# Top-2 experts: up weights copied four tiles ahead, rows transposed six and gathered nine tiles ahead

## What is computed

```python
gate_logits = xf @ gate_w.T
weights, indices = jax.lax.top_k(gate_logits, TOP_K)
weights = jax.nn.softmax(weights, axis=-1)
combine = jnp.zeros((N, E)).at[jnp.arange(N)[:, None], indices].add(weights)
out = jnp.zeros_like(xf)
for e in range(E):
    h = jax.nn.silu(xf @ w1[e].T) * (xf @ w3[e].T)
    y = h @ w2[e].T
    out = out + combine[:, e:e + 1] * y
```

## Time and profile before

| what | value |
|---|---|
| median of 3 runs | 778.28 us (776.01 to 778.66) |
| profiled execution, its own time | 781.1 us |
| its span, first to last instruction | 779.3 us |
| mean granted TensorE clock | 0.787 of full |
| busy, PE / PEld / DVE / ACT / POOL | 68% / 54% / 50% / 45% / 45% |
| the top-2 loop, first gather to last scatter issued | 527.4 to 753.6 us |
| read-back, weighing and store behind it | to 779.3 us |

### The profile page before, as it was taken

One profiled execution on the slowest core, in us unless ns is written; L12 is line 12 of the kernel. 1 busy time (PEld: TensorE's weight loads), 2 busy tenths in 40 slices (PEclk: granted clock), 3 DMA queues, 4 the chain that ended last, 5 costly groups with the idle time before them and its releaser, 6 DMA issues.

```text
span 779.3 us, 12795 instructions
## 1 busy us (share of the span) xinstructions
PE 526.4 (68%) x4449; PEld 419.5 (54%) x4449; DVE 389.9 (50%) x1030; ACT 346.9 (45%) x731; POOL 350.3 (45%) x343
## 2 busy tenths in 40 slices
PE   4999732215394755059999989756787878878750
PEld 2445531211153634037777768745787877867750
DVE  5365657788520112398999998582111111111117
ACT  1112135534331121037777773305665756666645
POOL 2000000000268887347888873005666666667630
PEclk9999855556787687558999995556998989999985
DMA  9701146000045463720000002343111111111129
GB/s 302 317 27 28 40 86 162 0 0 0 17 125 116 95 143 35 177 49 2 3 3 3 3 2 69 82 101 106 45 45 41 42 42 45 41 42 48 39 70 284
DMA packets 65245, 56.05 MB, mean 72 GB/s; under 512 B 10176, under 2 KB 59200, under 8 KB 65056
## 3 DMA queue, kind: packets, MB, share of 16 engines
q1 hardware_dynamic: 49904, 38.46, 17.3%
q0 software_dynamic: 10688, 14.04, 8.2%
q10 hardware_dynamic: 4592, 2.75, 1.3%
HBM read 35.38 MB, written 19.86 MB: 71 GB/s over the span
## 4 chain that ended last, share of the span: by engine, by line
PE 37%; POOL 16%; DVE 15%; issue 14%; ACT 9%; DMA 5%; another core or an unknown queue 3%; ACTq 1%; POOLq 0%; DVEq 0%; SPq 0%
PE psum L1605 8%; PE psum L1342 7%; POOL arena L553 6%; PE psum L1611 6%; PE psum L1621 5%; PE psum L1321 4%; ACT arena_b L1272 2%; POOL scratch L499 2%; ACT arena_b L1157 2%; POOL v_x L543 2%; POOL y_even L509 2%; POOL x_tok L536 2%; POOL x_tok L560 2%; ACT arena_b L1155 1%
## 5 line engine op out<-in xcount | busy, mean ns | idle before, releaser
L1082 DVE TENSOR_TENSOR arena<-arena,psum 128x384 f32<-128x384 f32 x71 | 39.3, 554 | 182.6 <-PE psum L1611 86.3
L499 POOL DMA_INDIRECT scratch<-table,idx x32 | 33.7, 1054 | 210.6 <-DVE idx_w L839 201.1
L576 POOL DMA_INDIRECT arena<-normed,gather_i x71 | 73.8, 1040 | 63.7 <-DVE gather_i L1058 41.9
L584 POOL DMA_INDIRECT results<-arena,dest_i x71 | 72.9, 1026 | 58.8 <-ACT arena L1294 45.4
L1605 PE MATMUL psum<-arena,arena_b 128*128 128x128 f32 x426 | 72.6, 312 | 38.7 <-ACT arena_b L1272 25.3
L1605 PEld LDWEIGHTS psum<-arena,arena_b 128*128 128x128 f32 x426 | 60.0, 213 | 45.7 <-ACT arena_b L1272 29.2
L553 POOL TENSOR_TENSOR arena<-arena,peak 128x1024 f32<-128x1024 f32 x32 | 60.9, 1903 | 30.2 <-DVE peak L927 30.2
L1272 ACT COPY arena_b<-w_sb 128x768 f32 x71 | 58.7, 826 | 23.9 <-issue 23.9
L1342 PE MATMUL psum<-scratch,conv_sb 128*128 128x512 f32 x144 | 65.0, 606 | 0.0
L1611 PE MATMUL psum<-arena,arena_b 128*128 128x128 f32 x426 | 65.0, 293 | 0.0
L1321 PE MATMUL psum<-cst,arena 128*128 128x128 f32 x327 | 58.4, 295 | 8.1 <-DMA arena<-normed,gather_i 6.9
(11 more groups left out here) (249 smaller groups left out, 1125.4 us busy)
## 6 DMA issues: line engine op xcount, KB each, us to landing
arena<-in_w_down_dram SPq DMA_DIRECT2D x8, 768.0 KB
w_sb<-in_w_dram SPq DMA_DIRECT2D x3, 1536.0 KB, 12.8
x_tok<-in_x_dram SPq DMA_DIRECT2D x4, 512.0 KB, 8.0
y_odd<-zeros SPq DMA_DIRECT2D x4, 512.0 KB
table<-xn SPq DMA_DIRECT2D x8, 256.0 KB, 2.3
y_even<-x_tok SPq DMA_DIRECT2D x16, 128.0 KB
extra<-y_odd ACTq DMA_DIRECT2D x4, 512.0 KB, 11.7
x_tok<-y_even SPq DMA_DIRECT2D x4, 512.0 KB, 10.6
```

Source lines behind the costliest of these rows:

```text
L499: nc.gpsimd.indirect_dma_start(out=rows_b[:, e // 4 % 4, e % 4, :], out_offset=None, in_=table[:, :], in_offset=bass.IndirectOffsetOnAxis( ...
L576: nc.gpsimd.indirect_dma_start(out=rows_d[:, t % ROWS_D, :], out_offset=None, in_=normed[:, :], in_offset=bass.IndirectOffsetOnAxis(ap=gat ...
L584: nc.gpsimd.indirect_dma_start(out=results[:, :], out_offset=bass.IndirectOffsetOnAxis(ap=dest_i[:, t:t + 1], axis=0), in_=yx_d[:, t % OUT ...
L1082: nc.vector.tensor_tensor(act_d[:, b, :], silu_d[:, b, :], psum[:, 4 + b, 0:FF_D], ALU.mult).then_inc(e_act, 1)
```

## The change

Five things are changed.

1. tile_weights runs four tiles ahead of the loop's index instead of three, so the copy for tile t+4 stands right behind silu(t+2). Its ring keeps its three buffers, and the copy waits for e_h3 of the tile three before it. Since the two weight copies no longer come in turn by tile, they get a semaphore each (e_w, e_w2).
2. X_AHEAD goes from 4 to 6: in iteration t TensorE transposes the rows of tile t+6, and evac_y(t) carries them out of PSUM. So up(t) waits for evac_y(t-6) instead of evac_y(t-4).
3. Nine gathers instead of six stand ahead of GpSimd's loop, and iteration t issues gather(t+9).
4. up(0) and up(1) stand behind rows_t(3) and rows_t(4), and rows_t(5) behind them.
5. On ScalarE silu(0), tile_weights(3) and silu(1) stand between the first row copies.

```diff
-X_AHEAD = 4
+X_AHEAD = 6
+GATHERS_AHEAD = 9
+FIRST_UPS = [3, 4]
...
-            AHEAD = 6
-            for t in range(AHEAD):
+            for t in range(GATHERS_AHEAD):
                 gather(t)
             pool.wait_ge(d_idx, 2)
             for t in range(RUN_D):
-                if t + AHEAD < RUN_D:
-                    gather(t + AHEAD)
+                if t + GATHERS_AHEAD < RUN_D:
+                    gather(t + GATHERS_AHEAD)
                 if t > 0:
                     scatter(t - 1)
...
                 nc.scalar.copy(w2_t[:, t % 4], w2_sb[:, bass.ds(e, 1), :, :]
-                               .rearrange("p e k h -> p (e k) h")).then_inc(e_w, 1)
+                               .rearrange("p e k h -> p (e k) h")).then_inc(e_w2, 1)
...
                 first_rows(t)
-            for t in range(2):
-                silu(t)
+                if t in FIRST_UPS:
+                    silu(FIRST_UPS.index(t))
+                if t == FIRST_UPS[0]:
+                    tile_weights(3)
             for t in range(RUN_D):
                 if t + 2 < RUN_D:
                     silu(t + 2)
+                if t + 4 < RUN_D:
+                    tile_weights(t + 4)
                 if t + 3 < RUN_D:
-                    tile_weights(t + 3)
                     down_weights(t + 3)
                 evac_y(t)
...
-                pe.wait_ge(e_w, 2 * t + 1)
+                pe.wait_ge(e_w, t + 1)
...
-                pe.wait_ge(e_w, 2 * t + 2)
+                pe.wait_ge(e_w2, t + 1)
...
             for t in range(X_AHEAD):
                 rows_t(t)
-            for t in range(2):
-                up(t)
+                if t in FIRST_UPS:
+                    up(FIRST_UPS.index(t))
```

More of the change, by code:

```diff
@@ L389, in metaformer @@
         f_scaled = sem("f_scaled")
-        e_tr, e_xt, e_h1, e_h3, e_silu, e_act, e_yp, e_y, e_w, d_wout = (
-            sem(f"e_{s}") for s in ("tr", "xt", "h1", "h3", "silu", "act", "yp", "y", "w", "wout"))
+        e_tr, e_xt, e_h1, e_h3, e_silu, e_act, e_yp, e_y, e_w, e_w2, d_wout = (
+            sem(f"e_{s}") for s in ("tr", "xt", "h1", "h3", "silu", "act", "yp", "y", "w", "w2", "wout"))
         e_ld = [sem(f"e_ld{i}") for i in range(ROWS_D)]
```

## The result

The changed kernel takes 772.25 us (median of 11 runs, 769.26 to 777.71) where the kernel before took 778.66 (11 runs beside it, 775.57 to 784.72). The ratio is 0.9921, 95% interval 0.9898 to 0.9945: faster by 0.8%, or 6.4 us. Forecast were 15 us and 763.3; the result lies in the range of 744 to 780, on the side of the case without change. The profiled execution has a span of 771.8 us against 779.3.

The account below looks back on a forecast made before the run. No engine was full; late signals and GpSimd's pauses held the loop, with GpSimd's 2.68 us a tile as floor. Fewer pauses (9.6 us) and the gathers (4.0) gave 13.6, or 18.4 at best; 15 us was taken: 763.3 us, range 744 to 780.

Parts of the forecast that it names:

- TensorE's side: Waits before the loop's first up matmuls: 32.6 of 38.4 us go, 5.8 stay; with 7 us of clock, about 40 could go.
- The 7 us of low clock: Up groups slowed to 1.65 us after five long TensorE waits, as the clock had fallen; 7 us more could go.
- The three gathers: Three gathers leave GpSimd's work between first and last scatter, 3 x 1.34 = 4.0 us saved.
- The start: Ahead of the loop, two transposes and one weight copy move forward: taken as 0, bounds -0.8 and +0.8 us.
- the term for GpSimd's pauses: GpSimd's idle waits for evac_y, 28.7 us: a pause each six tiles instead of four, of the old size, saves 9.6 us.
- the upper value of 14.4: Saving in us from GpSimd's pauses if one came each eight tiles; with 4.0 for the gathers, 18.4 us.
- Scatters idle 15 to 23 us: Sign for the forecast: GpSimd's scatters still idle that long for evac_y; under 4 us if the floor is reached.
- The last scatter near 738: Sign for the forecast: GpSimd issues its last scatter near 738 us in the trace, near 718 in the floor case.
- Silus late by over 3 us: Sign on ScalarE that lateness grew, if Silus still start that late.
- the slower rival: Signal delay grows with GpSimd's longer runs, TensorE waits longer: 6 us slower, 784 us; chance 0.08.
- The floor at 744: Rival: late signals keep their own pace, margins absorb them, GpSimd's issuing bounds the loop; gain 34 to 36.8 us; chance 0.30.
- no change: Rival: something TensorE and GpSimd share is full, each removed wait returns as a longer one; 776 to 781 us; chance 0.12.

## Why the prediction was right or wrong

**TensorE's side was read rightly as far as its waits go, and the sum did not rest on it.** That the weights' margin would take up the waits of about zero to 2.23 us holds, and so does that the longer ones would shrink: ahead of its groups TensorE waits about 9 us, none over 1.1, where the term left 5.8. But another 20 us of standing still inside groups have come, for which the prediction had no term, so 29.0 us remain. The 7 us of low clock did not come back either: 0.91 against 0.92. That the weights' margin would be of no use without X_AHEAD 6 is right for TensorE's waits (36.4 us with it alone) and wrong for the time, of which it alone gave 4.6 us.

**The three gathers** are the term that held: 133 intervals became 130, 4.0 us. The claim beside it, that eleven gathers fit ahead of the first scatter, holds too: the last one is over at 540.1, 14.3 us behind the start of the first, where the first scatter stood 15.2 us behind it. But evac_y of the first tile itself comes later now, so the first scatter starts at 543.79. The start was taken as 0, at most +0.8, and cost 2.83 us from the first gather on: a second term that was off. With the old order of the start it is 17.9 us from the first gather to the first scatter, as against 18.0, so the early up groups aren't the reason; the run of eleven issues, with signals late from its middle on, may be.

**The step that failed is the term for GpSimd's pauses, 9.6 us: "each still ends in a pause of the old size".** From the first to the last scatter there were 211.03 - 133 x 1.34 = 32.8 us beyond the bare issues, and now there are 201.67 - 130 x 1.34 = 27.5. The term is 5.3 us, not 9.6, and the upper value of 14.4 was further off. The number of pauses thinned out nearly as forecast: waits for evac_y fell from 27 to 20 (without the first in each case), to 0.74 of what they were, where the forecast was 4/6 (though they stood each 2.6 tiles, not each fourth). But each grew from 1.36 to 1.63 us: (41.6 - 4.8) / 27 and (36.2 - 3.7) / 20. Less 0.30 for the usual step between issues, the old size would have left 28.7 x 20 / 27 = 21.3 us; the new one leaves 32.5 - 20 x 0.30 = 26.5. So 5.2 of the 7.4 us that the smaller number gave were lost to the size. The other 3.1 of the 5.3 lie in the streams' ends, outside the two windows, and in short steps without a named releaser. The runs did not grow to ten or twelve: but for two of ten they are eight or fewer, and eight nearly everywhere, where before many were six, four or two.

Why a run stays eight, and why its pause is longer: it ends when a scatter needs a down group whose signal is held. The change gave margin to the weights and the rows, the two inputs of the up group. It gave none to the path from up group to Silu, product and down group, which all wait for held signals; VectorE's product alone waits up to 6.0 us for one. TensorE can be two tiles ahead there, as before. This is argued from the rows; a kernel with the up groups three tiles ahead was not tried.

**The signs.** Fewer waits at the first up group than 23: wrong, 27, though short. Scatters idle 15 to 23 us: wrong, 36.2. Runs of ten or more: wrong. The last scatter near 738: wrong, 745.46, about halfway to before's 753.63. Few up groups of 1.65 us: wrong, 15 first up groups take 1.5 us or more, by low clock or by standing still inside, where 6 did before. Transposes do not wait for gathered rows in the loop: right, and with six gathers ahead they would. Silus late by over 3 us as the sign that lateness grew: 24 of 71, so the mechanism of the slower rival is there, its point of decision (4.7 us of wait for six tiles) is not reached.

**The rivals.** The floor at 744 rested on signals that come late at their own pace, which the plain scatters refute. That something shared by TensorE and GpSimd is full, which stood under "no change", is nearest to what the runs show; I gave it 0.12, and its time of 776 to 781 leaves out the 4 us of the gathers and the 5 of the pauses, less the 2.8 that the start cost. The assumption under the forecast, that lateness belongs to long runs of GpSimd issues, is right in kind, but not enough alone, as the kernel with six gathers shows. What was wrong was to take the pauses' size as fixed while the margins grew.

## What to carry over

Where two engines' times overlap and one's signals are late while the other issues indexed transfers back to back, margins mostly move the waits: look whether what is told late is on the loop's own path, and give margin there or take issues away. Count the pauses of the engine that is waited for, and their size, before pricing a margin; both may change. A substitute that computes something else but keeps the matmuls (here plain for indexed scatters, -59 us) shows in one run what a suspected coupling is worth, before any is spent on working around it.

## What the runs showed of the hardware

TensorE's completion signals come up to 7.6 us late, and in the change TensorE stands still inside matmul groups, by up to 1.1 us, while GpSimd issues indexed gathers or scatters of 128 rows each 1.34 to 1.49 us. This needs a TensorE that is free to run on: where it waited 47.2 us for gathered rows (six gathers ahead), no signal that a Silu waits for was over 1.2 us late, though GpSimd issued each 1.34 us in runs of up to eight. At 2.12 us between indexed issues signals are prompt behind the loop's first tiles, also with a plain transfer of GpSimd (0.58 us, 0.88 with the step behind it) between each two, and with a memset of 1024 columns there. At 1.55 us, with a gap of 1.1 us in each four, they are prompt too, but there TensorE was also held up by its gathers, so it isn't known whether the spacing, the gap, or the slower TensorE did it. Whether the signal or the group's own end comes late can't be told either, since the profile models the ends of matmuls. How the two are coupled the traces don't show, nor whether the data type or the number of rows matters; both are left open.
